# Reordering the 64-key attentions: scores between the two halves of the transposes, keys and queries in a PSUM bank of their own

## The chip, the cores and the metric

One Trainium2 chip, of which the kernel uses one core. The metric is the device time of one execution, in microseconds. The kernel before takes 2080.19 us, the median of 3 runs (2080.02 to 2080.28).

## The reference, cut to what matters

Four layers run over the same 64 batches of 64 tokens of width 128, in float32: a transformer layer with relative positions over 128 keys, a layer with self-attention, cross-attention and feed-forward, a gated fusion with the pooled context, and a layer with self-attention, cross-attention and a mixture of experts. What the change touches are four attentions with 16 heads of 8 channels and 64 keys each:

```
q = heads(q_in, wq, bq)
k = heads(kv_in, wk, bk)
v = heads(kv_in, wv, bv)
scores = jnp.einsum('bhqd,bhkd->bhqk', q, k) / jnp.sqrt(jnp.float32(dh))
attn = jax.nn.softmax(scores, axis=-1)
out = jnp.einsum('bhqk,bhkd->bhqd', attn, v)
```

The first ("msa") and the third ("sa") are self-attentions on the normed tokens; the second ("ca1") and the fourth ("ca") take keys and values from the context. The first and the second have a mask; the third and the fourth have biases on query and key. The output of each is projected and added to the tokens.

## The kernel before, in words

The kernel is one program with phases; each of the five engines has a program of its own, written out by hand, and they meet between phases. Semaphores with counts order the engines within a phase. The four attentions run in two phases of two attentions each (`att_tensor`, `att_vector`, `att_scalar`, `att_pool`, `att_sync`). A tile is two batches of 64 tokens, so 128 partitions; each attention has 32 tiles. `walk_pair` lets both attentions of a phase run on without a break, as a software pipeline: in the step of tile n each engine does, in the order of the code, the `head` work of tile n+2 (norm, transposes, projections), the `front` work of tile n+1 (scores, maximum, shift, exponent), the `back` work of tile n (transposes of the probabilities, product with the values) and the `late` work of tile n-1 (transpose of the context, output projection, addition to X). The steady steps are in a loop of two.

TensorE's order in a step is: the first half of the transposes of tile n's probabilities (`transpose_probs`, line 861, into PSUM bank 4), the second half (bank 5), the mask and scores of n+1 (lines 878 and 883, banks 0 to 3), the transpose of the normed tile n+2 (892) and of its context tile (896 or 899), both into bank 6, the product with the values of n (906, bank 5), the transpose of the context of n-1 (915, bank 6), the products for query, key and values of n+2 (923, 924, 927, all in bank 7), the output projection of n-1 (932, bank 6).

ScalarE copies the two halves of transposed probabilities (1027), the transposed tiles (1039, 1041), computes the first half of the exponents of n+1 (1021), copies the transposed context (1048), the query and the key together (1056 with bias, 1058 without), computes the second half of the exponents, and copies the values (1066).

VectorE norms tile n+2 (962 to 974), finds the maximum (983) and subtracts it (985) in two halves for n+1, takes the reciprocal (990) and multiplies the context (993) of n, adds the projected output to X (999) for n-1 and takes moments (271, 275).

GpSimd makes the mask (830), adds the bias to X (836, 838), and spreads the key over four masked copies (842), which the scores need. SyncE issues the loads of context tiles (805) and masks (809).

## Time and profile before

| what | value |
|---|---|
| median of 3 runs | 2080.19 us |
| the profiled execution | 2078.7 us |
| its span | 2077.1 us |
| busy: TensorE, its weight loads, VectorE, ScalarE, GpSimd | 80%, 62%, 66%, 55%, 46% of the span |
| granted clock of TensorE, mean | 0.905 of full speed |
| line 842 on GpSimd | 128 times, 1048 ns, 299.6 us idle in front of it |
| line 861 on TensorE, transposes | 1024 times, 33.4 us idle in front of them |
| line 983 on VectorE | 256 times, 53.3 us idle in front of it, for the scores |

Busy time leaves out waits and the issuing of DMAs. Idle time is that of the engine just before an instruction, with the engine whose work released it. Times in the rows below are microseconds from the start of the span.

### The profile page before, as it was taken

The numbers are of one execution on the slowest core, as the hardware profiler recorded it, in microseconds if no ns is written. First come the engines' busy times: TensorE is split into PE (matmuls) and PEld (weight loads), VectorE is DVE, ScalarE is ACT, GpSimd is POOL, SyncE is SP. The second block draws the span as 40 slices with busy tenths as digits, with TensorE's granted clock in tenths as the row PEclk, the third lists the DMA queues.
The fourth block names the chain that finished last, engine by engine and source line by source line (L and its number), as shares of the span: only waits on it lengthen the run. The fifth ranks groups of instructions, "written<-read, shape, count | busy, mean of one in ns | idle before, by whom it ended". The sixth has DMA issues, their size and how long they took to land. (4 is left out here: it accounts for less than half of the span.)

```text
span 2077.1 us, 56431 instructions
## 1 busy us (share of the span) xinstructions
PE 1656.3 (80%) x17626; PEld 1290.7 (62%) x17626; DVE 1377.0 (66%) x4296; ACT 1139.2 (55%) x3291; POOL 960.6 (46%) x1443
## 2 busy tenths in 40 slices
PE   5899999999996799998887844599988862219882
PEld 5788888888875666666665721366666651217771
DVE  2677777777775478877776459677777752127783
ACT  1677777777763255566664412377777740007771
POOL 1444444444433344556664424444444434435773
PEclk9999999999998899999998967699999975559996
DMA  6776666666650222210000000000000000016665
GB/s 184 146 161 146 150 145 150 150 152 147 139 127 11 75 88 98 89 52 16 15 15 6 0 1 0 3 0 0 3 11 11 11 5 29 27 51 209 212 221 155
DMA packets 214507, 166.84 MB, mean 80 GB/s; under 512 B 27344, under 2 KB 188496, under 8 KB 214160
## 3 DMA queue, kind: packets, MB, share of 16 engines
q1 hardware_dynamic: 205840, 142.85, 27.5%
q0 software_dynamic: 8576, 22.88, 3.2%
q8 instruction: 45, 0.74, 0.2%
q14 instruction: 46, 0.38, 0.1%
HBM read 91.92 MB, written 73.76 MB: 80 GB/s over the span
## 5 line engine op out<-in xcount | busy, mean ns | idle before, releaser
L842 POOL TENSOR_TENSOR sb_work<-sb_work,sb_cols 128x512 f32<-128x512 f32 x128 | 134.1, 1048 | 299.6 <-ACT sb_work L1056 190.9
L701 ACT ACTIVATE sb_probs<-sb_probs,sb_work 128x128 f32<-128x128 f32 x512 | 198.5, 405 | 112.7 <-DVE sb_work L626 112.7
L983 DVE TENSOR_REDUCE sb_work<-PS 128x8 f32<-128x512 f32 x256 | 175.4, 685 | 53.3 <-PE PS L883 53.3
L280 POOL TENSOR_SCALAR sb_next_var_eps<-sb_next_moments 128x1 f32<-128x1 f32 (+1 forms) x184 | 43.3, 235 | 322.4 <-DVE sb_next_moments L275 322.1
L1021 ACT ACTIVATE sb_work<-sb_work 128x512 f32<-128x512 f32 x256 | 161.2, 630 | 56.2 <-DVE sb_work L985 55.9
L861 PE MATMUL PS<-sb_ident,sb_work 128*128 128x128 f32 x1024 | 165.0, 285 | 33.4 <-ACT sb_work L1021 28.0
L985 DVE TENSOR_TENSOR sb_work<-PS,sb_work 128x512 f32<-128x512 f32 x256 | 177.1, 692 | 8.8
L861 PEld LDWEIGHTS PS<-sb_ident,sb_work 128*128 128x128 f32 x1024 | 114.4, 143 | 68.3 <-ACT sb_work L1021 55.0
L906 PE MATMUL PS<-sb_v_ones,sb_work 128*64 128x18 f32 x4096 | 144.6, 213 | 1.9 <-ACT sb_work L1027 1.8
L906 PEld LDWEIGHTS PS<-sb_v_ones,sb_work 128*64 128x64 f32 x4096 | 132.2, 139 | 19.6 <-issue 7.3
L1027 ACT ACTIVATE sb_work<-PS 128x512 f32<-128x512 f32 x256 | 139.4, 595 | 4.7 <-PE PS L861 1.5
L430 POOL TENSOR_TENSOR sb_work<-sb_rel_bias,sb_work 128x2064 f32<-128x2064 f32 x32 | 134.7, 4211 | 5.2 <-POOL sb_work L428 4.2
L284 POOL TENSOR_TENSOR sb_tile_inv_std<-sb_next_var_eps,sb_half_power 128x1 f32 (+3 forms) x184 | 121.1, 658 | 8.5 <-issue 0.4
L554 PE MATMUL PS<-sb_VO,sb_pkvT 128*128 128x128 f32 x1024 | 119.9, 275 | 0.6 <-ACT sb_pkvT L712 0.6
L554 PEld LDWEIGHTS PS<-sb_VO,sb_pkvT 128*128 128x128 f32 x1024 | 116.9, 192 | 2.7 <-ACT sb_pkvT L712 2.7
L1800 POOL DMA_INDIRECT expert_outs<-sb_work x92 | 94.7, 1029 | 50.4 <-issue 39.7
L535 PE MATMUL PS<-sb_probsT,sb_kv_in 128*128 128x512 f32 x256 | 115.6, 594 | 0.9 <-DVE sb_probsT L648 0.9
L626 DVE CUSTOM_DVE_ANT_0 sb_probs<-PS,sb_work 128x128 f32<-128x128 f32 x512 | 112.4, 285 | 5.6 <-DMA sb_work<-rel_scratch 5.6
L1039 ACT ACTIVATE sb_work<-PS,sb_cols 128x128 f32<-128x128 f32 x128 | 55.1, 455 | 94.0 <-PE PS L899 48.3
L641 DVE TENSOR_TENSOR sb_work<-PS,sb_work 128x512 f32<-128x512 f32 x128 | 82.2, 684 | 34.1 <-PE PS L569 28.9
L701 ACT ACTIVATION_READ_ACCUMULATOR sb_probs<-sb_probs,sb_work 128x1 f32 x512 | 104.1, 203 | 0.0
L734 ACT ACTIVATE sb_work<-PS 128x512 f32<-128x512 f32 x128 | 76.3, 598 | 46.6 <-PE PS L1147 35.8
(274 smaller groups left out, 4477.6 us busy)
## 6 DMA issues: line engine op xcount, KB each, us to landing
rel_scratch<-sb_work SPq DMA_DIRECT2D x64, 516.0 KB, 7.8
sb_work<-rel_scratch SPq DMA_DIRECT2D x64, 512.0 KB, 6.6
expert_rows<-sb_blank SPq DMA_DIRECT2D x36, 520.0 KB, 2.9
sb_w_up<-expert_halves SPq DMA_DIRECT2D x23, 512.0 KB
sb_w_down<-expert_halves SPq DMA_DIRECT2D x23, 512.0 KB
expert_halves<-sb_e_halves POOLq DMA_DIRECT2D x16, 512.0 KB, 5.9
sb_work<-expert_rows SPq DMA_DIRECT2D x23, 260.0 KB
sb_e_raw<-e_W POOLq DMA_DIRECT2D x16, 256.0 KB, 6.7
```

What stands on the lines that cost most here:

```text
L284: e.tensor_tensor(inv_std[:, bass.ds(t0, tiles)], var_eps[:, 0:tiles], half_power[:, 0:tiles], ALU.pow)\
L430: e.tensor_tensor(masked_bias, rel_bias[:, :, :], mask_f.unsqueeze(1).to_broadcast([P, H, KL + 1]), ALU.add)\
L535: e.matmul(PS[:, (j + 1) % 4], kv_in[:, u, b], probsT[:, 8 * G:8 * G + 8, S * b:S * b + S], start=True, stop=True).then_inc(sem("l0_pkv_do ...
L554: ins = e.matmul(PS[:, 3, 0:D], pkvT[:, j], VO[:, j], start=(j == 0), stop=(j == H - 1))
L701: ins = e.activation(probs[:, j], probs[:, j], ACT.Exp, bias=neg_max[:, j:j + 1], scale=-1.0, accum_out=row_sum[:, j:j + 1])
L842: e.tensor_tensor(k_masked[:, u], k_sb[:, u].rearrange("p (b k) -> p b k", b=2).unsqueeze(2) .to_broadcast([P, 2, 4, S]), col("place").uns ...
L861: ins = e.transpose(PS[:, 4 + j, i * P:i * P + P], att_probs[:, u, 8 * j + 2 * i:8 * j + 2 * i + 2], ident[:, :])
L906: ins = e.matmul(values[S * b:S * b + S, 2 * i:2 * i + 2], att_probsT[:, i, S * b:S * b + S], v_ones[:, u, b, 2 * i:2 * i + 2], start=True ...
L983: e.tensor_reduce(top, mine, AX.X, ALU.max).then_inc(sem("att_max_ready"), 1)
L985: e.tensor_tensor(by_group(att_probs[:, v])[:, 2 * j:2 * j + 2], mine, top.unsqueeze(3).to_broadcast([P, 2, 4, S]), ALU.subtract)\
L1021: e.activation(att_probs[:, v, 8 * j:8 * j + 8], att_probs[:, v, 8 * j:8 * j + 8], ACT.Exp, scale=front["scale"]).then_inc(sem("att_exp_do ...
L1027: e.activation(att_probsT[:, 4 * j:4 * j + 4].rearrange("p i q -> p (i q)"), PS[:, 4 + j], ACT.Copy)\
```

## The change

Five edits, of which each moves or splits work and none adds any arithmetic.

1. TensorE: the mask and scores of tile n+1 go between the first and the second half of the transposes of tile n.
2. TensorE: query and key of tile n+2 go into bank 4, the key first, with a count `att_qk_done` of their own behind them; the values stay in bank 7. The bank is shared with the first half of the transposes, so these wait until query and key have been copied.
3. ScalarE copies the key first and the query second when `att_qk_done` says so, each with a count, and waits for the values only before it copies these.
4. GpSimd makes the masked keys after the key's copy; the scores wait for the query's copy as well.
5. TensorE transposes the context of tile n-1 in front of the transposes of tile n+2 and of the product with values; ScalarE copies it in front of the copies of the transposed tiles, and waits until these transposes are done, since they go to the same bank.

```diff
@@ att_pool
-                    e.wait_ge(sem("att_qk_kept"), m + 1)
+                    e.wait_ge(sem("att_qk_kept"), 2 * m + 1)
@@ att_tensor
                 if back:
+                    if front:
+                        e.wait_ge(sem("att_qk_kept"), 2 * n + 4)
                     transpose_probs(n, u, 0)
-                    wait(e, sem("att_ctx_ready"), n)
-                    transpose_probs(n, u, 1)
                 if front:
                     c, m, v = front, n + 1, 1 - u
                     e.wait_ge(sem("att_k_masked"), m + 1)
+                    wait_alone(e, sem("att_qk_kept"), 2 * m + 2)
                     wait(e, sem("att_shifted"), 2 * m)
...
                     ins.then_inc(sem("att_scores_done"), 1)
+                if back:
+                    wait(e, sem("att_ctx_ready"), n)
+                    transpose_probs(n, u, 1)
+                if late:
+                    e.wait_ge(sem("att_ctx_ready"), n)
+                    if head or front:
+                        e.wait_ge(sem("att_T_kept"), n + 2)
+                    wait_alone(e, sem("att_added"), n - 1)
+                    e.transpose(PS[:, 6, 2 * P:3 * P], att_ctx[:, 1 - u], ident[:, :]).then_inc(sem("att_ctxT_done"), 1)
...
-                if late:
-                    e.wait_ge(sem("att_ctx_ready"), n)
-                    if head:
-                        e.wait_ge(sem("att_T_kept"), n + 3)
-                    wait_alone(e, sem("att_added"), n - 1)
-                    e.transpose(PS[:, 6, 2 * P:3 * P], att_ctx[:, 1 - u], ident[:, :]).then_inc(sem("att_ctxT_done"), 1)
                 if head:
...
-                    wait(e, sem("att_qk_kept"), m)
+                    wait(e, sem("att_qk_kept"), 2 * m)
+                    wait(e, sem("att_probsT_kept"), 2 * n + 1 if back else 0)
                     wait(e, sem("att_v_ready"), m)
                     src = yT if cross is None else cT
-                    e.matmul(PS[:, 7, 0:P], wq, yT[:, u], start=True, stop=True)
-                    e.matmul(PS[:, 7, P:2 * P], wk, src[:, u], start=True, stop=True)
+                    e.matmul(PS[:, 4, P:2 * P], wk, src[:, u], start=True, stop=True)
+                    e.matmul(PS[:, 4, 0:P], wq, yT[:, u], start=True, stop=True)\
+                        .then_inc(sem("att_qk_done"), 1)
@@ att_scalar
+                if late:
+                    e.wait_ge(sem("att_ctxT_done"), n)
+                    if head:
+                        e.wait_ge(sem("att_transposed"), n + 3)
+                    wait(e, sem("att_out_done"), n - 2)
+                    e.activation(att_ctxT[:, 1 - u], PS[:, 6, 2 * P:3 * P], ACT.Copy).then_inc(sem("att_ctxT_kept"), 1)
...
-                if late:
-                    e.wait_ge(sem("att_ctxT_done"), n)
-                    wait(e, sem("att_out_done"), n - 2)
-                    e.activation(att_ctxT[:, 1 - u], PS[:, 6, 2 * P:3 * P], ACT.Copy).then_inc(sem("att_ctxT_kept"), 1)
                 if head:
                     c, m = head, n + 2
-                    e.wait_ge(sem("att_projected"), m + 1)
+                    e.wait_ge(sem("att_qk_done"), m + 1)
...
-                    for i, (to, of) in enumerate(((q_sb, PS[:, 7, 0:P]), (k_sb, PS[:, 7, P:2 * P]))):
+                    for i, (to, of) in ((1, (k_sb, PS[:, 4, P:2 * P])), (0, (q_sb, PS[:, 4, 0:P]))):
...
-                    ins.then_inc(sem("att_qk_kept"), 1)
+                        ins.then_inc(sem("att_qk_kept"), 1)
                 if front:
                     exponent(1)
                 if head:
+                    e.wait_ge(sem("att_projected"), m + 1)
```

## Rows read from the trace of the kernel before

**Rows 1.** Timeline, third attention, one step: start, duration, engine, instructions merged
```profile
1434.66 0.69 PE L883 MATMUL PS<-sb_work 32*64 32x256 f32 x16
...
1435.55 1.11 PE L906 MATMUL PS<-sb_v_ones,sb_work 128*64 128x18 f32 x32
...
1436.59 0.33 PE L915 MATMUL PS<-sb_ident,sb_work 128*128 128x128 f32 x1
...
1436.76 0.39 PE L923 MATMUL PS<-sb_work,sb_w_sa 128*128 128x128 f32 x2
...
1436.98 0.39 PE L924 MATMUL PS<-sb_work,sb_w_sa 128*128 128x128 f32 x2
...
1437.30 0.66 PE L927 MATMUL PS<-sb_w_sa,sb_work 128*64 128x128 f32 x8
...
1438.00 0.62 ACT L1056 ACTIVATE sb_work<-PS,sb_cols 128x128 f32<-128x128 f32 x2 [0.30 <-PE PS L927]
...
1438.79 1.05 POOL L842 TENSOR_TENSOR sb_work<-sb_work,sb_cols 128x512 f32<-128x512 f32 x1 [2.82 <-ACT sb_work L1056]
...
1439.20 0.66 PE L861 MATMUL PS<-sb_ident,sb_work 128*128 128x128 f32 x4 [0.39 <-ACT sb_work L1021]
...
1439.63 1.08 ACT L1027 ACTIVATE sb_work<-PS 128x512 f32<-128x512 f32 x2
...
1439.97 0.69 PE L883 MATMUL PS<-sb_work 32*64 32x256 f32 x16
...
1440.59 0.33 PE L892 MATMUL PS<-sb_ident,sb_work 128*128 128x128 f32 x1
```

**Rows 2.** Timeline, first scores of the first attention, TensorE idle until then
```profile
721.13 1.05 POOL L842 TENSOR_TENSOR sb_work<-sb_work,sb_cols 128x512 f32<-128x512 f32 x1
...
722.24 1.04 PE L878 MATMUL PS<-att_mask,sb_ident 128*128 128x256 bf16 x4 [3.86 <-POOL sb_work L842]
```

**Rows 3.** Timeline, first attention, a long step and the ends around it
```profile
759.98 0.69 PE L883 MATMUL PS<-sb_work 32*64 32x256 f32 x16
...
762.13 0.39 PE L923 MATMUL PS<-sb_work,sb_w_msa 128*128 128x128 f32 x2
...
763.90 1.05 POOL L842 TENSOR_TENSOR sb_work<-sb_work,sb_cols 128x512 f32<-128x512 f32 x1 [2.19 <-ACT sb_work L1058]
...
763.99 0.28 DVE L999 TENSOR_TENSOR sb_X<-sb_X,PS 128x128 f32 x1
...
765.18 0.60 PE L878 MATMUL PS<-att_mask,sb_ident 128*128 128x256 bf16 x4
...
765.71 0.69 PE L883 MATMUL PS<-sb_work 32*64 32x256 f32 x16
...
766.88 0.32 PE L892 MATMUL PS<-sb_ident,sb_work 128*128 128x128 f32 x1 [0.49 <-DVE sb_work L974]
...
768.35 0.39 PE L923 MATMUL PS<-sb_work,sb_w_msa 128*128 128x128 f32 x2
...
770.12 0.29 DVE L999 TENSOR_TENSOR sb_X<-sb_X,PS 128x128 f32 x1
```

**Rows 4.** Timeline, second attention, from the projections to the next tile's copies
```profile
1036.20 0.39 PE L923 MATMUL PS<-sb_work,sb_w_ca 128*128 128x128 f32 x2
...
1036.48 0.28 ACT L1048 ACTIVATE sb_work<-PS 128x128 f32<-128x128 f32 x1
...
1039.17 0.33 SPq L805 DMA_DIRECT2D sb_work<-ctx  x1
...
1041.04 0.33 PE L899 MATMUL PS<-sb_ident,sb_work 128*128 128x128 f32 x1 [0.31 <-DMA sb_work<-ctx]
...
1041.56 0.46 ACT L1039 ACTIVATE sb_work<-PS,sb_cols 128x128 f32<-128x128 f32 x1 [1.58 <-PE PS L899]
```

**Rows 5.** Timeline, fourth attention, the copies in front of the projections
```profile
1604.72 0.81 ACT L1039 ACTIVATE sb_work<-PS,sb_cols 128x128 f32<-128x128 f32 x2 [1.00 <-PE PS L896]
...
1605.77 0.45 PE L923 MATMUL PS<-sb_work,sb_w_ca 128*128 128x128 f32 x2
```

## The prediction

> **What bounds the kernel now.** I read the page's shares first: no engine is full over the span, so what counts is the four attentions, 32 tiles each. The rows that group instructions show idle time of TensorE in front of the transposes (line 861), of GpSimd in front of the masked keys (842) and of ScalarE in front of its copies. A sum of idle time says nothing of order, so I went to the timeline of a steady step in each attention. Call P the start of the key and query products (923/924).
>
> In the third attention a step takes 5.31 us, scores to scores [rows 1]. One loop closes on that number: from P 1.20 us until the value products end (1436.76 to 1437.96); 0.04 to the two copies of query and key (1438.00); 1.20 to the second half of the transposes (1439.20), in which ScalarE finishes the pair and computes the second exponent, for which TensorE is idle 0.39; 0.77 to the scores (1439.97), 3.21 so far. Then 0.62 to the next transpose, 0.27 to the product with values (1435.55, 0.89 after the scores at 1434.66), 1.04 to the context transpose, 0.17 to P: 2.10. The sum is 5.31. The reader is to see that the masked keys run beside the second exponent and end at 1439.84, only 0.13 before the scores: the loop has a twin, P to copies to GpSimd to scores, of nearly the same length. VectorE has room here.
>
> The first attention has a short and a long step, 5.73 (scores at 759.98 and 765.71) and 6.22 (P at 762.13 and 768.35). In the long one the transpose of the normed tile (892) waits for VectorE's norm [rows 3]. In the second attention the chain goes through the addition to X, the moments of the context, the load of the next context tile and its transpose (899): P 1036.20, load issued 1039.17, transposed 1041.04 [rows 4]. With 0.26 to the product with values, 1.05 and 0.17 that is 6.32 a step. The fourth alternates too, and its longer step waits for the norm in the same place as the first.
>
> **The change part by part.** Nothing is computed anew; the same instructions change places, three waits are split or added, and no DMA is moved. Each path has to be walked again in the new order: first half of transposes, scores, second half, context transpose, normed tile's transpose, product with values, P, value products, output.
>
> Keys and queries in a bank of their own: ScalarE may copy when line 924's place ends, P+0.61 (1436.98+0.39), not P+1.20; and the key goes first with its own count, so GpSimd starts after one copy, not two. Copies overlap by some 0.10 (0.46 for one of a kind that takes 0.81 for two [rows 4, 5]), so in the pair of 0.62 each lasts 0.36 and holds ScalarE for 0.26; the second costs 0.26. Line 842 moves from P+2.03 to 2.03-0.59-0.26 = P+1.18 and ends at P+2.23 [rows 1]. Before the first scores, when TensorE had nothing else, it started 0.06 after 842 ended [rows 2]. Behind that wait there now stands one more (queries kept) with an instruction of its own, which no row shows. Lower bound 0.06; upper bound 0.28, the 0.11 between transposes and scores (1439.86 to 1439.97) plus the 0.17 that GpSimd took after ScalarE's pair (1438.62 to 1438.79). I take 0.10, since the queries are kept long before, at P+1.27, and only issue remains. Scores start at P+2.33, not P+3.21. Ahead of them on TensorE the first half now waits for the kept queries, about P+1.32; the value products in front of it last until P+1.20 and the output's product comes behind them, so this wait is hidden or nearly so, with nothing to spare: a later copy would delay the first half, and then has some 0.3 of cover until the masked keys come.
>
> Scores between the halves: this takes away the cover that the scores gave to the copy of the second half. From the start of the second half the product with values can't come sooner than 0.66 (transposes) + 0.04 + 0.60 (copy) + 0.05 = 1.35 later; what lies between is the context transpose 0.17 and the normed tile's 0.26, so TensorE stands some 0.2 here [rows 1]. The new loop of the third attention: P+2.33 scores, +0.62 second half, +1.35 product with values, +1.05 P. Together 5.35, against 5.31: the loop is shorter by the exponent and the wait for the value products, and longer by line 842, which ran beside the exponent, and by the copy that has lost its cover. 32 x 0.04 = 1.3 us lost. The exponents are no longer in it: the second is done near P+1.8 and wanted at P+2.95.
>
> In the masked attentions 0.53 us of mask matmuls stand before the scores (765.18 to 765.71), and copies without bias: 842 starts at P+1.77 now (762.13 to 763.90), 0.26 sooner than in the third; since one of the two copies goes, I keep 0.18 of that, an estimate. The loop is 5.35+0.53-0.18 = 5.70; the short step, 5.73 now, therefore stays. The long step goes P, addition +1.77 (768.35 to 770.12), transpose of the normed tile +2.89 (763.99 to 766.88), product with values +0.26, P +1.05: 5.97, against 6.22 [rows 3]. The context transpose has left this path (0.17), and VectorE no longer waits for scores, which come 0.9 sooner. 16 x 0.25 = 4.0 us gained.
>
> Context transposed sooner: it saves 0.17 between the product with values and P, wherever the front of the step sets the pace. But its copy on ScalarE (0.28 at 1036.48, and 0.18 until the next can start, by the 0.10 that copies overlap) now stands in front of the copies of the transposed tiles, and waits until those transposes are done. In the second attention these copies start 0.52 after the last transpose (1041.04 to 1041.56) [rows 4]. The new P is 0.52+0.18+0.36+0.27+0.05 = 1.38 after that transpose; TensorE itself would be ready at 0.26+1.05 = 1.31; now it is 1.48. The gain is 0.10 a step, 32 x 0.10 = 3.2 us. In the fourth attention the two copies scale and add: 0.81 from 1604.72. P = 1604.72+0.18+0.81+0.05 = 1605.76, against 1605.77 [rows 5]: nothing gained, and by the same path nothing in its short step.
>
> A rule of the Trainium skill bears on this (PSUM — Partial Sum Buffer, "PSUM bank collisions raise a hardware error"): two engines may not touch one bank in the same partitions at once, so a copy of the context must not run while TensorE transposes into its bank. That is what the added wait keeps to. Nothing in this trace shows two engines in one bank, so no row bears the rule out or speaks against it. Were the copy free to go ahead, the sum would gain the 2.2 and 4.6 us of rival (b); with the wait it is the one below.
>
> **Sum.** First 4.0, second 3.2, third -1.3, fourth 0: 5.9 us. The profiled execution lasted 2078.7 us with a span of 2077.1; the median is 2080.19, 1.5 above it, and the terms are differences of steps, so I subtract them there: 2074.3. Ends of the attentions give a few tenths at most (the first tile's copies come 0.6 sooner) and are left out.
>
> **The rivals.** (a) *The mask path is longer than I think: slower.* If x is added to the 2.33, the third attention pays 32x, the first's short steps 16x, the fourth's short steps 16 times what exceeds 0.12. The gain is used up at x = 0.12; at the upper bound x = 0.18 it costs 9.6, time 2083.9; a slip of 0.3 would cost 17 and give 2091. For it: both new waits stand directly in this loop, and the queries' wait has no slack. Against it: when TensorE stood idle, it went on within 0.06.
>
> (b) *Larger gain.* ScalarE's copies come through in time: second attention 0.07 x 32 = 2.2, fourth 0.17 x 16 + 0.12 x 16 = 4.6, and with a wait of 0.06 another 1.9. Total 8.7 more, time 2065.6. For it: starts of small copies overlap. Against: the 0.52 seen after the transpose.
>
> (c) *It does nothing that can be measured.* The loads of the second attention and the norm of the first keep their pace: the latter's 4.0 goes, or the second's 3.2, and 2 to 3 us stay: 2077.7. For it: each of the old loops has a twin of nearly equal length. Less than 0.2%, 4.2 us, is about what a measurement can't tell from no change.
>
> (d) *GpSimd holds up VectorE.* Line 842 moves 0.85 sooner, over VectorE's reciprocal, context and addition. In the first attention it ran beside the addition already (763.90 and 763.99) and that took 0.28 as usual [rows 3]; so I give it a twentieth. If it doubled each addition (0.28 more), the norm path would be that much later: some 48 steps, 13 us, time 2088.
>
> **How the numbers follow.** My forecast, 2070 to 2077, has 0.38; (a) 0.20; (b) 0.17; (c) 0.20; (d) 0.05. Faster by over 0.2% (under 2076.0) holds the first and (b), less what of the forecast falls just short: 0.52. Within: (c) and the mild part of (a), 0.27. Slower (over 2084.3): 0.21, the rest of (a), and (d). The forecast's own range is 2070 to 2077. The range goes from (b)'s 2065 to 2086, past the upper bound of (a).
>
> **What would show it.** Right: 842 starts near P+1.0 and P+1.2; scores start 0.1 after it ends; TensorE's idle time in front of the first-half and second-half transposes for ScalarE's exponent is gone, and new idle time stands before the scores (for GpSimd) and before the product with values (for the copies). Steps: first 5.85 on average, second 6.2, third 5.35, fourth 5.78. Wrong: third attention over 5.5 (mask path), or the fourth well under 5.78 (copies), or lines 993 or 999 longer than 0.3.

## The result: slower by 0.85%

The changed kernel takes 2099.26 us (median of 4 runs, 2097.13 to 2101.37), the kernel before 2080.24 beside it; the ratio is 1.0085, with an interval of 1.0066 to 1.0104. The forecast was 2074.3 and the range ended at 2086.0: the sign, the number and the range are all wrong. The profiled execution took 2097.13 us with a span of 2095.5, 18.4 more than before.

From the first scores of each attention to its last (31 steps), from the score rows of both timelines:

| attention | before | after | difference | forecast |
|---|---|---|---|---|
| first | 185.8 us, 5.99 a step | 190.8, 6.15 | +5.0 | -4.0 |
| second | 194.3, 6.27 | 198.1, 6.39 | +3.8 | -3.2 |
| third | 165.6, 5.34 | 175.1, 5.65 | +9.5 | +1.3 |
| fourth | 179.9, 5.80 | 186.3, 6.01 | +6.4 | 0 |

The four sum to +24.7; the stretches before, between and behind them give back 6.3, and 18.4 is left.

Groups of instructions of the kernel after (busy time, mean ns of one, idle time of the engine in front and what ended it):

```profile
L842 POOL TENSOR_TENSOR sb_work<-sb_work,sb_cols 128x512 f32<-128x512 f32 x128 | 134.3, 1049 | 229.9 <-ACT sb_work L1064 154.4
L1033 ACT ACTIVATE sb_work<-PS 128x512 f32<-128x512 f32 x256 | 152.8, 597 | 160.4 <-PE PS L861 156.0
L989 DVE TENSOR_REDUCE sb_work<-PS 128x8 f32<-128x512 f32 x256 | 174.4, 681 | 23.3 <-PE PS L884 23.0
L916 PE MATMUL PS<-sb_v_ones,sb_work 128*64 128x18 f32 x4096 | 142.5, 212 | 33.5 <-ACT sb_work L1033 32.7
L884 PE MATMUL PS<-sb_work 32*64 32x256 f32 x2048 | 91.0, 411 | 16.5 <-POOL sb_work L842 16.5
L879 PE MATMUL PS<-att_mask,sb_ident 128*128 128x256 bf16 x256 | 39.1, 275 | 26.5 <-POOL sb_work L842 26.5
```

By what is idle where, the change did what it says. GpSimd idles 230 us in front of the masked keys, not 299.6; VectorE idles 23 for the scores, not 53.3. TensorE's 33.4 us in front of the transposes have gone (0.8 left), but 33.5 us now stand in front of the product with values (before: 1.9), for ScalarE's copy, and this copy waits 160 us for its transposes (before: 4.7). And a second wait is new: in front of the scores and of the mask's products TensorE idles 16.5 and 26.5 us, all of it for the masked keys; in the kernel before it was 8.2 and 13.0, of which 1.9 and 3.9 for them. The idle time in these four places together went from 56.5 to 77.3 us. Sums of idle time don't show an order, so the step's timeline has to show where the loop went. Third attention of the kernel after:

```profile
1433.02 0.49 PE L928 MATMUL PS<-sb_work,sb_w_sa 128*128 128x128 f32 x2
...
1433.34 0.39 PE L929 MATMUL PS<-sb_work,sb_w_sa 128*128 128x128 f32 x2
...
1433.77 0.62 ACT L1064 ACTIVATE sb_work<-PS,sb_cols 128x128 f32<-128x128 f32 x2 [0.91 <-PE PS L929]
...
1434.21 1.05 POOL L842 TENSOR_TENSOR sb_work<-sb_work,sb_cols 128x512 f32<-128x512 f32 x1 [2.29 <-ACT sb_work L1064]
...
1435.56 0.69 PE L884 MATMUL PS<-sb_work 32*64 32x256 f32 x16 [0.29 <-POOL sb_work L842]
...
1436.18 0.66 PE L861 MATMUL PS<-sb_ident,sb_work 128*128 128x128 f32 x4
...
1436.88 0.60 ACT L1033 ACTIVATE sb_work<-PS 128x512 f32<-128x512 f32 x1 [0.89 <-PE PS L861]
...
1437.62 1.11 PE L916 MATMUL PS<-sb_v_ones,sb_work 128*64 128x18 f32 x32 [0.49 <-ACT sb_work L1033]
...
1438.66 0.49 PE L928 MATMUL PS<-sb_work,sb_w_sa 128*128 128x128 f32 x2
```

Follow P (1433.02) round to the next P (1438.66). 842 starts at P+1.19, where the forecast had 1.18. It ends at 1435.26 and the scores start 0.30 later. Then 0.62 to the second half, 0.70 to its copy, 0.74 to the product with values (0.60 of copy and 0.14 behind it), 1.04 to P. The sum is 5.64, the forecast's was 5.35. This is the forecast's own loop, link by link, with two links that it made too short: 0.10 for the wait behind 842, and 0.05 behind the copy. The wait of 0.30 in this step is a long one. Over 27 steps it is 0.25 on average, and 842 starts at P+1.23 on average; the sum is again 5.64.

First attention, the same loop with the mask's products in it:

```profile
764.89 0.49 PE L928 MATMUL PS<-sb_work,sb_w_msa 128*128 128x128 f32 x2
...
765.99 1.05 POOL L842 TENSOR_TENSOR sb_work<-sb_work,sb_cols 128x512 f32<-128x512 f32 x1 [1.81 <-ACT sb_work L1066]
...
767.44 0.60 PE L879 MATMUL PS<-att_mask,sb_ident 128*128 128x256 bf16 x4 [0.40 <-POOL sb_work L842]
...
767.97 0.69 PE L884 MATMUL PS<-sb_work 32*64 32x256 f32 x16
...
771.07 0.49 PE L928 MATMUL PS<-sb_work,sb_w_msa 128*128 128x128 f32 x2
```

P to P is 6.18 here, forecast 5.70; of the 0.48 the wait has 0.30. Over 27 steps the average is 6.13, which is 0.43 more than forecast: 0.26 in the wait behind 842 (0.36), 0.08 between the start of the second half and the product with values, and 0.10 in front of 842, which starts at P+1.10 where the forecast's sum had 1.00. Every step now runs on this loop, the long ones as the short ones: the 6.22 of [rows 3] came down a little, and the 5.73 went up by 0.4.

In the second attention the early copy of the context works, but not all of its gain arrives:

```profile
1037.79 0.33 PE L909 MATMUL PS<-sb_ident,sb_work 128*128 128x128 f32 x1 [0.37 <-DMA sb_work<-ctx]
...
1038.23 0.28 ACT L1040 ACTIVATE sb_work<-PS 128x128 f32<-128x128 f32 x1 [0.40 <-PE PS L909]
...
1038.77 0.27 ACT L1053 ACTIVATE sb_work<-PS 128x128 f32<-128x128 f32 x1
...
1039.28 0.46 PE L928 MATMUL PS<-sb_work,sb_w_ca 128*128 128x128 f32 x2
```

The context tile is transposed 1.49 before P (forecast 1.38; before, 1.48 in [rows 4]). The last copy ends at 1039.04 and the first product follows 0.24 later, not 0.05. The way from P to the load has grown too: the addition to X starts at P+1.84 (1032.93 to 1034.77), in the kernel before at P+1.77 (1036.20 to 1037.97). The step from P to P is 6.35 here, and the average over the attention 6.39; what lies between these two wasn't followed up.

Last, a thing that the prediction hasn't in any term. Windows of the fourth attention, kernel after (length; busy time and count of TensorE, its weight loads, VectorE, ScalarE and GpSimd; granted clock, where 1.00 is full speed; DMA):

```profile
1618.00:1623.00 5.00, 3.92 (x64) 2.78 (x62) 3.23 (x9) 3.55 (x10) 2.42 (x5) 1.00 0.05 13
1623.00:1627.00 4.00, 4.00 (x34) 2.99 (x34) 1.86 (x7) 2.11 (x7) 1.05 (x1) 0.57 0.00 0
1627.00:1633.00 6.00, 5.50 (x90) 3.82 (x75) 4.53 (x12) 4.66 (x12) 2.58 (x6) 1.00 0.04 11
```

For some 4 us TensorE's granted clock is about half, the lower of its two levels (1.2 GHz and not 2.4); it was idle for 1.1 of the 5.0 us before that. There are four such stretches from 1620 to 1702, and steps in which one begins take 6.7 to 7.3 us. The kernel before has one in its fourth attention, twice as long (at 1533, in a step of 8.12 us). What the four cost is estimated below, from a kernel without them, at 2 to 4 us.

### The profile page after: what moved, and what is told of

Read it like the earlier page. It is cut to its first block and busy times, and to the rows that moved or that the text cites. A ratio compares the mean times of both kernels' runs of the same rounds, so it can differ in the third digit from the quotient of the medians.

```text
span 2095.5 us, 56958 instructions
## 1 busy us (share of the span) xinstructions
PE 1648.3 (79%) x17626; PEld 1293.5 (62%) x17626; DVE 1370.2 (65%) x4296; ACT 1139.1 (54%) x3291; POOL 964.5 (46%) x1443
## 5 line engine op out<-in xcount | busy, mean ns | idle before, releaser
L1033 ACT ACTIVATE sb_work<-PS 128x512 f32<-128x512 f32 x256 | 152.8, 597 | 160.4 <-PE PS L861 156.0
L1027 ACT ACTIVATE sb_work<-sb_work 128x512 f32<-128x512 f32 x256 | 161.7, 632 | 17.0 <-DVE sb_work L991 16.5
L916 PE MATMUL PS<-sb_v_ones,sb_work 128*64 128x18 f32 x4096 | 142.5, 212 | 33.5 <-ACT sb_work L1033 32.7
L884 PE MATMUL PS<-sb_work 32*64 32x256 f32 x2048 | 91.0, 411 | 16.5 <-POOL sb_work L842 16.5
L734 ACT ACTIVATE sb_work<-PS 128x512 f32<-128x512 f32 x128 | 76.2, 598 | 44.7 <-PE PS L1156 34.0
```

The source lines that it names most:

```text
L916: ins = e.matmul(values[S * b:S * b + S, 2 * i:2 * i + 2], att_probsT[:, i, S * b:S * b + S], v_ones[:, u, b, 2 * i:2 * i + 2], start=True ...
L1027: e.activation(att_probs[:, v, 8 * j:8 * j + 8], att_probs[:, v, 8 * j:8 * j + 8], ACT.Exp, scale=front["scale"]).then_inc(sem("att_exp_do ...
L1033: e.activation(att_probsT[:, 4 * j:4 * j + 4].rearrange("p i q -> p (i q)"), PS[:, 4 + j], ACT.Copy)\
```

## Experiments

Each kernel was run beside the kernel before (2080.31, 2078.84 and 2083.53 us in the three sessions), and the ratios are to that. "Half-clock time" below is the time at the lower clock in 735 to 1105 and 1345 to 1675 us of the span. It leaves out one stretch of some 30 us (48 with the scores alone) that every kernel here has just ahead of the third attention (in the kernel before from 1308 to 1339, so outside these windows), and of which a few us fall into the window from 1345 in the slower kernels. Each kernel has one profile, so step lengths and half-clock times are those of one execution.

**The bank alone.** Edits 2 to 4 of the change, with the scores and the context's transpose where the kernel before has them.

```diff
-                    e.matmul(PS[:, 7, 0:P], wq, yT[:, u], start=True, stop=True)
-                    e.matmul(PS[:, 7, P:2 * P], wk, src[:, u], start=True, stop=True)
+                    e.matmul(PS[:, 4, P:2 * P], wk, src[:, u], start=True, stop=True)
+                    e.matmul(PS[:, 4, 0:P], wq, yT[:, u], start=True, stop=True)\
+                        .then_inc(sem("att_qk_done"), 1)
```

> Only keys and queries in their own bank, copied early, key first; both halves of the transposes stay ahead of the scores and the context is transposed where it was. Loop theory (every step is set by one loop of waits, and what the change lost was cover): in the third attention the second exponent now waits only for VectorE's shift, 3.53 us after the scores' start, plus 0.05, 0.63 and 0.05, and the scores follow 0.77 after the second half: a step of 5.03 instead of 5.31, 9 us gained there; 2 us in the first, the second and fourth unchanged: about 2069 us. Rival theory (the bank shared with the first half of the transposes and the added waits are what cost the 18 us): at or above the kernel before, 2080 to 2095 us.

Measured: 2096.76 us, ratio 1.0075 (1.0057 to 1.0094), just above the rival's range. But the loop theory's step came: the third attention is down to 5.10, near the 5.03 expected; yet the whole is slower. The second attention takes 6.80 on average with a median of 6.40. The windows say why:

```profile
735.00:920.00 185.00, 162.59 (x2343) 122.72 (x2342) 144.97 (x363) 113.61 (x308) 93.39 (x185) 0.96 0.23 87
920.00:1105.00 185.00, 160.95 (x2086) 121.06 (x2087) 129.35 (x356) 107.79 (x300) 116.37 (x271) 0.91 0.06 15
1345.00:1510.00 165.00, 148.43 (x2206) 111.40 (x2207) 128.16 (x309) 122.35 (x311) 76.22 (x151) 0.96 0.00 1
1510.00:1675.00 165.00, 145.67 (x2013) 109.68 (x2012) 121.29 (x303) 117.86 (x302) 68.73 (x139) 0.93 0.04 11
```

A clock of 0.91 over 185 us is some 32 us at half speed. The first, second and fourth window hold 70 us in 20 stretches, most of some 4 us. The 0.96 of the third window is something else: it is the end of the long stretch ahead of the third attention, which here runs from 1329 to 1359; the steady steps behind it have the full clock. The kernel before has 1.00, 1.00, 1.00 and 0.98 in these windows. One of the stretches, with the step before it:

```profile
1016.05 0.66 PE L932 MATMUL PS<-sb_w_ca,sb_work 128*64 128x128 f32 x8
...
1018.44 0.69 PE L886 MATMUL PS<-sb_work 32*64 32x256 f32 x16
1020.16 0.32 PE L895 MATMUL PS<-sb_ident,sb_work 128*128 128x128 f32 x1 [1.03 <-DVE sb_work L969]
...
1023.06 1.12 PE L932 MATMUL PS<-sb_w_ca,sb_work 128*64 128x128 f32 x8
...
1026.24 0.69 PE L886 MATMUL PS<-sb_work 32*64 32x256 f32 x16
```

In this step TensorE waits once, for the norm, and its slack is one gap of 1.03 us; in the kernel before the longest gap of a step of this attention is 0.28 in the median and 0.65 at most. Behind it the clock falls, the value products take 1.12 instead of 0.66, and the step is 7.80 long. The gap alone doesn't explain the fall, though: of the ten falls in this attention five come in steps that have two gaps of 0.38 to 0.51 instead, and eight steps with one gap of 0.90 to 1.05 have none.

**The scores alone.** Edit 1 and nothing else.

```diff
                 if back:
                     transpose_probs(n, u, 0)
-                    wait(e, sem("att_ctx_ready"), n)
-                    transpose_probs(n, u, 1)
                 if front:
...
                     ins.then_inc(sem("att_scores_done"), 1)
+                if back:
+                    wait(e, sem("att_ctx_ready"), n)
+                    transpose_probs(n, u, 1)
```

> Only the scores between the two halves of the transposes; keys and queries stay in the values' bank and are copied late. Loop theory: the masked keys end at P+3.08, the scores start 0.3 later, and then 0.62 + 0.70 + 0.74 + 1.04 + 0.17 follow to the next P: 6.65 in the third and fourth attention, 6.97 in the first and second. That is 43 + 28 + 32 + 22 us: about 2205 us. Rival (the mask product is hidden and only the waits' number counts): within 10 us of the kernel before, 2075 to 2090 us.

Measured: 2228.97 us, ratio 1.0707 (1.0681 to 1.0732), 24 above the 2205 expected. The undisturbed steps are 6.85, 6.85, 6.48 and 6.48, somewhat shorter than expected. Third attention:

```profile
1438.23 1.05 POOL L842 TENSOR_TENSOR sb_work<-sb_work,sb_cols 128x512 f32<-128x512 f32 x1 [3.65 <-ACT sb_work L1057]
...
1439.42 0.69 PE L881 MATMUL PS<-sb_work 32*64 32x256 f32 x16 [1.17 <-POOL sb_work L842]
...
1445.89 0.69 PE L881 MATMUL PS<-sb_work 32*64 32x256 f32 x16 [1.16 <-POOL sb_work L842]
```

TensorE stands 1.17 for the masked keys, and steps of 9.2 us at half clock come on top, in the third and fourth attention. So the scores between the halves need the early keys. The wait behind 842 is 0.14 here, and 0.24 in front of the mask's products, with the semaphores of the kernel before.

The second attention of this kernel says something of the clock. TensorE stands 0.82 to 1.01 for the masked keys in every step of the window below, in most of them 1.00:

```profile
980.34 0.60 PE L876 MATMUL PS<-att_mask,sb_ident 128*128 128x256 bf16 x4 [1.00 <-POOL sb_work L842]
```

Its window, with the columns as above:

```profile
920.00:1105.00 185.00, 144.95 (x2096) 106.83 (x2096) 128.33 (x346) 105.21 (x294) 111.39 (x256) 1.00 0.07 20
```

TensorE is idle 40 of these 185 us, the bank alone 24, and yet the clock is 1.00 throughout. Neither a gap of some 1 us in each step nor a smaller share of busy time was enough to bring it down here.

**The context alone.** Edit 5 and nothing else.

```diff
+                if late:
+                    e.wait_ge(sem("att_ctx_ready"), n)
+                    if head or front:
+                        e.wait_ge(sem("att_T_kept"), n + 2)
+                    wait_alone(e, sem("att_added"), n - 1)
+                    e.transpose(PS[:, 6, 2 * P:3 * P], att_ctx[:, 1 - u], ident[:, :]).then_inc(sem("att_ctxT_done"), 1)
                 if head:
```

> Only the context transposed and copied sooner. Loop theory: the context transpose in front of P hid 0.10 of the loading of the first weights, so moving it takes 0.07 and not 0.17 out of the path from the product with values to P, while it adds its 0.17 ahead of the normed tile's transpose where the scores set the pace: third attention 5.41 (+3 us), the others within 1 us each: about 2083 us. Rival (the copy of the context in front of the copies of the transposed tiles is what costs most): the second and fourth attention slower by 0.1 to 0.2 a step, 2088 us or more.

Measured: 2074.15 us, ratio 0.9969 (0.9957 to 0.998): faster by 0.31%, where 2083 was expected. Steps 5.92, 6.20, 5.37 and 5.78 on average. The second attention's 6.20 is the forecast's 6.2, the first's long step came from 6.22 to 6.11, and the other two are what they were. No half-clock time. Here P follows the last copy of the transposed tiles after 0.05 us wherever TensorE waits for it, the forecast's figure; this kernel doesn't have the wait that edit 2 adds in that place.

**The masked keys' wait put last.** The whole change, with the order of the waits in front of the scores turned round.

```diff
-                    e.wait_ge(sem("att_k_masked"), m + 1)
-                    wait_alone(e, sem("att_qk_kept"), 2 * m + 2)
+                    e.wait_ge(sem("att_qk_kept"), 2 * m + 2)
                     wait(e, sem("att_shifted"), 2 * m)
                     if c["mask"]:
                         e.wait_ge(sem("att_mask_ready"), m + (c["mi"] - c["i"]) * NT + 1)
+                    wait_alone(e, sem("att_k_masked"), m + 1)
```

> The whole change, but TensorE waits for the kept queries, the shift and the mask first and for the masked keys last, in an instruction of its own, so that nothing stands behind the wait that ends last. Theory (the 0.30 to 0.35 between the end of line 842 and the scores is the issuing of the waits behind it): that gap falls to 0.15 or less, steps of the third attention from 5.64 to 5.45 or so, 16 to 20 us less in all attentions bound by it with the second less: 2086 to 2092 us. Rival (the gap is the way of GpSimd's signal to TensorE): gap and time unchanged, 2097 to 2100 us.

Measured: 2096.89 us, ratio 1.008 (1.0061 to 1.0099). Expected were 2086 to 2092, so the time missed. From the end of 842 to TensorE's next product, medians of the third and of the first attention: 0.14 and 0.24 in the kernel before, 0.24 and 0.36 in the whole change. Here it takes two values in turn, step by step: 0.14 and 0.25 in the third, 0.10 and 0.25 in the first. A step of the short kind:

```profile
1440.04 1.05 POOL L842 TENSOR_TENSOR sb_work<-sb_work,sb_cols 128x512 f32<-128x512 f32 x1 [2.34 <-ACT sb_work L1065]
...
1441.23 0.69 PE L885 MATMUL PS<-sb_work 32*64 32x256 f32 x16
```

So in every second step the order of the waits is worth 0.10 us in the third attention and 0.26 in the first, and in the others nothing in the third and 0.10 in the first; why every second step keeps 0.25 is open. On average the wait went from 0.25 to 0.20 and from 0.36 to 0.17. The third attention's steps followed, 5.65 to 5.61, and the first's only in part, 6.15 to 6.03, since in the steps with the short wait the product with values waits longer (0.28 behind the copy, not 0.14). The time fell by 2 us, within the intervals. The order of the waits is a part of the loss, and a small one.

**The bank alone, with unread work in the gap.** As the first experiment, and four transposes of the identity behind the scores in the first, second and fourth attention, into a place of bank 7 that nobody reads then. They change no result.

```diff
+                    if head and back and c["i"] != 2:
+                        e.wait_ge(sem("att_v_ready"), m + 1)
+                        for i in range(4):
+                            e.transpose(PS[:, 7, 0:P], ident[:, :], ident[:, :])
```

> The bank-only kernel with four transposes of the identity, that nobody reads, on TensorE behind the scores in the first, second and fourth attention, written to the free quarter of bank 7. Work is added, none taken away. Clock theory (in the bank-only kernel all of TensorE's slack of a step stands in one gap of 1.03 us in front of the normed tile's transpose, and behind such a gap the granted clock falls to the lower level for some 4 us; 23 such stretches are what made it slower): with about 0.5 us of the gap filled the stretches are gone, and what is left are the steps, 5.94, 6.37, 5.07 and 5.85: about 2076 us, 20 us less than without the added work. Rival (the shared bank and the waits cost the time, and the clock only follows): no fewer stretches, and the time rises by the added work where it stands in the loop, 2097 to 2110 us.

Measured: 2074.11 us, ratio 0.9969 (0.9957 to 0.9981): 22.6 us less than without, by adding work, and near the 2076 expected. The windows that answer to those above:

```profile
735.00:920.00 185.00, 177.45 (x2523) 133.61 (x2522) 149.86 (x373) 115.87 (x315) 96.05 (x191) 1.00 0.24 87
920.00:1105.00 185.00, 172.90 (x2315) 129.03 (x2313) 135.00 (x375) 112.53 (x316) 123.07 (x289) 0.99 0.06 16
1345.00:1510.00 165.00, 152.94 (x2357) 116.61 (x2357) 136.23 (x328) 128.34 (x327) 78.67 (x160) 1.00 0.01 2
```

The medians of the steps are those of the kernel without these transposes within 0.1 us (6.38 and 6.40 in the second attention, 4.94 in both in the third); what has gone are the slow steps. Two stretches of half clock are left, 7 us in all, where there were 20. The third window, whose own attention got no such transposes, rose from 0.96 as well only because this kernel is ahead by then: its long stretch runs from 1309 to 1340 and ends before the window.

**Bank and context, scores not moved**, and **the same with the four transposes**. Edits 2 to 5 without edit 1.

> The change without its reordering of the scores: own bank and early copies, context transposed sooner, both halves of the transposes ahead of the scores. Loop theory, by the sum of the two parts measured alone (16.5 slower and 6.2 faster): 2090 us, with a step of 5.1 in the third attention and stretches at the lower clock as in the bank-only kernel, fewer if the context transpose, now inside the gap, splits it. If the reordering of the scores is what costs most of the change's 18 us beside the clock, this kernel beats the whole change; if not, it stands at 2097 or above.

Measured: 2084.73 us, ratio 1.0024 (1.0013 to 1.0034); steps 5.91, 6.72, 5.02, 6.04 and 62 us at half clock. The whole change differs from this kernel in edit 1 alone and takes 14.5 us more.

> The kernel of own bank and context sooner, with the same four unread transposes behind the scores. Clock theory: no stretches at the lower clock in the attentions except at their ends, steps of 5.9, 6.25, 5.1 and 5.8: about 2070 us, the fastest of all. Rival (the clock falls whatever the gaps): 2085 us or more.

Measured: 2067.58 us, ratio 0.9937 (0.9923 to 0.9951); steps 5.85, 6.45, 5.02, 5.83 and 7 us at half clock. Faster by 0.63% than the kernel before, and by 1.5% than the kernel after.

**The whole change with unread work.** Three such transposes behind the early transpose of the context, where it waits for ScalarE's copy.

```diff
+                    if head and back:
+                        e.wait_ge(sem("att_v_ready"), n + 2)
+                        for i in range(3):
+                            e.transpose(PS[:, 7, 0:P], ident[:, :], ident[:, :])
```

> The whole change with three unread transposes of the identity behind the context transpose, where TensorE waits for the norm or for the copy of the second half. Clock theory: the four stretches of some 4 us at the lower clock in the fourth attention go, which is about 4 us, and the steps stay, since the added 0.35 us lies beside waits of 0.5 to 0.6: 2094 to 2097 us. Rival (the change's loss is mostly the clock): 2080 to 2085 us.

Measured: 2094.82 us, ratio 1.0069 (1.0055 to 1.0083), as expected; no half-clock time, steps 6.14, 6.37, 5.65, 5.94. Mostly the fourth attention moved (from 6.01, 2.3 us over its 31 steps). The medians differ by 4.4 us, and the intervals overlap. So the clock holds at most some 4 us of the whole change's loss, and the other 15 are in its steps.

**Half the masked keys**, in the whole change and in the kernel before. Line 842 makes the masked keys of a tile's first batch only, and the scores of both batches are computed from them; the second batch's own keys are left out.

```diff
-                    e.tensor_tensor(k_masked[:, u], k_sb[:, u].rearrange("p (b k) -> p b k", b=2).unsqueeze(2)
-                                    .to_broadcast([P, 2, 4, S]),
-                                    col("place").unsqueeze(1).unsqueeze(3).to_broadcast([P, 2, 4, S]), ALU.mult)\
+                    e.tensor_tensor(k_masked[:, u, 0], k_sb[:, u, 0:S].unsqueeze(1).to_broadcast([P, 4, S]),
+                                    col("place").unsqueeze(2).to_broadcast([P, 4, S]), ALU.mult)\
...
-                            ins = e.matmul(scores[S * b:S * b + S, g], q_sb[r, v, S * b:S * b + S], k_masked[r, v, b],
+                            ins = e.matmul(scores[S * b:S * b + S, g], q_sb[r, v, S * b:S * b + S], k_masked[r, v, 0],
```

> The whole change, with line 842 making the four masked keys of a tile's first batch only (256 elements in each partition in place of 512, so some 0.5 us shorter); the scores of both batches use them, so the scores of the second batch are computed from the first batch's keys. Loop theory: in the whole change the step is one loop, products, copy of the key, masked keys, scores, second half, copy, product with values. Then cutting 0.5 us out of line 842 shortens the third attention's step from 5.64 until the next limit, 4.9 to 5.15, the first's short step from 6.13 to about 5.7, the second's hardly (6.3), the fourth's to about 5.8: in all some 25 us, time 2072 to 2080. Rival (the splits and added waits cost their own time, whatever the masked keys take): steps within 0.1 us of the whole change's, time 2092 to 2100.

Measured: 2093.12 us, ratio 1.0044 (1.0029 to 1.0058). Third attention:

```profile
1434.70 0.69 PE L883 MATMUL PS<-sb_work 32*64 32x256 f32 x16
...
1437.80 0.49 PE L927 MATMUL PS<-sb_work,sb_w_sa 128*128 128x128 f32 x2
...
1438.99 0.62 POOL L842 TENSOR_TENSOR sb_work<-sb_work,sb_cols 128x256 f32<-128x256 f32 x1 [1.90 <-ACT sb_work L1063]
...
1439.40 0.65 PE L860 MATMUL PS<-sb_ident,sb_work 128*128 128x128 f32 x4
...
1439.98 0.69 PE L883 MATMUL PS<-sb_work 32*64 32x256 f32 x16
```

842 lasts 0.43 less and the step is 5.28, 0.36 less than 5.64; the rival, that the added waits themselves cost the time, wanted no change. The next limit comes sooner than expected: the masked keys end at 1439.61, but TensorE issues the first half of the transposes at P+1.60 and needs 0.58 for it, so the scores can't start before P+2.18. The first attention's steps went from 6.15 to 5.86. The time, though, missed its 2072 to 2080 by far, because there are now some 27 us at half clock in the second attention (6.65 on average, median 6.31) and 31 in the fourth, up to 1700; the third has none. That was not foreseen in the expectation, in spite of the first experiment.

> The same cut of line 842 in the kernel before, nothing else changed. Loop theory: there the masked keys run beside the second exponent, which ends its own path to the scores at nearly the same time, so the cut gives next to nothing: third attention 5.25 to 5.35 a step (now 5.31), time 2077 to 2081. If line 842 was the limit in the kernel before as well, the third attention would come down to 5.1 or less and the time to 2070 or less.

Measured: 2077.27 us, ratio 0.9974 (0.9954 to 0.9994). Third attention:

```profile
1435.37 0.62 POOL L842 TENSOR_TENSOR sb_work<-sb_work,sb_cols 128x256 f32<-128x256 f32 x1 [2.86 <-ACT sb_work L1055]
...
1436.37 0.69 PE L882 MATMUL PS<-sb_work 32*64 32x256 f32 x16
...
1441.68 0.69 PE L882 MATMUL PS<-sb_work 32*64 32x256 f32 x16
```

5.31 as before, with the masked keys ready 0.38 ahead of the scores. The same cut that takes 0.36 off a step of the changed kernel takes nothing off this one: in the kernel before 842 lay beside the exponent, and the change put it on the only path. The first and the fourth attention gained 1.6 and 3.3 us; the fourth's may be the clock, since the one long step of the kernel before (8.12 us, at half clock) is missing here.

**A mix.** Context sooner in all four attentions; own bank, key first and early copies only in the first and third; scores not moved. Then the same with the four unread transposes in the first attention.

```diff
+                    early = head["i"] in (0, 2)
...
+                    if early:
+                        e.matmul(PS[:, 4, P:2 * P], wk, src[:, u], start=True, stop=True)
+                        ins = e.matmul(PS[:, 4, 0:P], wq, yT[:, u], start=True, stop=True)
+                    else:
+                        e.matmul(PS[:, 7, 0:P], wq, yT[:, u], start=True, stop=True)
+                        ins = e.matmul(PS[:, 7, P:2 * P], wk, src[:, u], start=True, stop=True)
```

> Own bank, early copies and key first only in the first and third attentions; context transposed sooner in all four; scores where the kernel before has them. The aim is the short third attention (about 5.0 a step) without the lower clock that the own bank brought in the second. Steps 5.9, 6.2, 5.0, 5.8: 2062 to 2070, some half-clock stretches possible in the first attention. If the clock falls in the first as it did in the second with the bank in all, 2070 to 2078.

Measured: 2072.72 us, ratio 0.9945 (0.9925 to 0.9965); steps 5.90, 6.35, 5.02, 5.95; some 10 us at half clock. A gain, 3 us short of the first expected range, since the second attention didn't keep the 6.20 it has with the context alone (it goes 6.54 and 6.25 in turn) and the fourth takes 5.95, not 5.8. The instructions of the second are the same; what differs are the counts it waits on and how it follows on the first. This stays open.

> The kernel of the run before with four more transposes behind the scores in the first attention, into a bank place that nobody reads; they go where TensorE waits anyway. Clock theory: any half-clock stretches of the first attention go, its steps 5.85, time 2060 to 2066. If there were none to begin with: the same time within 2 us or up to 2 us more.

Measured: 2069.89 us, ratio 0.9928 (0.9904 to 0.9953); no half-clock time up to 1675, the first attention at 5.84 as expected, the time 4 us above the expected 2060 to 2066. The interval overlaps those of the mix without unread work and of bank, context and unread transposes (0.9923 to 0.9951): these three are the best versions, 0.55 to 0.7% faster than the kernel before, and nothing here tells them apart.

## Why the prediction was wrong

**Right: where each loop goes.** The loop of the third attention is the predicted one link by link, P, key's copy, masked keys, scores, second half, its copy, product with values, P; 842 starts at P+1.19 against 1.18 (1.23 on average). Halving 842 in both kernels showed it to be on the path that sets the step after the change, and covered before it. Also right is the idle time that was to vanish and to appear. Of two errors in the 1.18, one made good the other: the key and query products take 0.32 and 0.39, not 0.22 and 0.39, since the context's transpose no longer stands in front of them (in the kernel with the context alone they start 0.32 apart too), and what follows was 0.09 shorter.

**Wrong: "I take 0.10, since the queries are kept long before, at P+1.27, and only issue remains."** Measured 0.30 in the step shown, 0.24 and 0.36 as medians of the third and first attention. The upper bound was 0.28. The 0.10 leant on [rows 2], TensorE idle for 3.86 us, and passed over [rows 3], in which the mask's products start at 765.18 and 842 ends at 764.95: 0.23, from a steady step, in a row that was quoted. That row alone doesn't prove the price, since TensorE's transposes ran until 765.05; the scores alone, where TensorE stood idle for 1.00 before it, show the same 0.24. So 0.14 and 0.24 is what the kernel before pays in steady steps, and the added wait brings 0.10 and 0.12 more. The queries are indeed kept long before; the wait on them costs all the same, because it stands behind the one that comes last: with that one put last the time falls to 0.14 and 0.10 in every second step. In the third attention's step shown this is 0.20 of the 0.29 by which the loop was mis-sized, and 0.15 on average.

**Wrong: 0.05 behind a copy that TensorE waits for.** The second half's copy cost 0.66+0.04+0.60+0.05 in the forecast. The product with values starts 0.14 after its end (the median of 30 steps), and 1.44 after the second half; that is another 0.09. No row of the prediction shows the 0.05 for this place. Behind the copy of the transposed tile, where a wait has been added too, it is 0.24 (0.05 in the kernel with the context alone, which doesn't have that wait), and takes the forecast's 0.10 a step from the second attention. In the kernel with the context alone 0.07 of them came.

Put in the forecast's own sums, rival (a)'s x, which is what the loop takes more than forecast, is 0.29 in the third (31 x 0.29 = 9.0, with the 1.3 foreseen 10.3; measured 9.5). In the first it is 0.43 on average, since the estimate "I keep 0.18 of that" was 0.10 too much as well; it lifts the mask's loop to 6.13, above the 5.97 of the norm's, so that the gain of 4.0 became a loss of 5.0. This is rival (a), at 0.20 and 2083.9 to 2091: the rival was right and its price too low, because the wait behind 842 was bounded at 0.28, the one behind the copy had no bounds at all, and (a) left the second attention out, which turned from a gain of 3.2 into a loss of 3.8. The loops of the second and the fourth attention (+6.4) weren't taken apart link by link.

**Missing: TensorE's clock.** No term and no rival had it; the table ahead of the prediction shows 0.905, but nearly all of that lies outside the attentions, where the kernel before has 1.00, 1.00, 1.00 and 0.98. In the whole change it is a small matter, at most 4 us. In the parts it decides the sign: the bank alone goes from 2074.11 to 2096.76 and bank with context from 2067.58 to 2084.73 where the unread transposes are taken out. With such transposes in both, edit 1 costs 2094.82 - 2067.58 = 27 us on top of the others; without them in either, 14.5.

**The other rivals.** (b) and (c) didn't come: in the kernel with the context alone, where the mask's path is as before, the second attention gained 2.0 of its 3.2, the first 2.2 of 4.0. (d) is refuted: the multiplication of the context (999) and the addition (1005) still take at most 0.293 and 0.289.

What the whole change got wrong as an idea follows. Edit 5 alone is a gain of 0.31%. Edits 2 to 5 together are a gain of 0.63% with unread work on TensorE, and a loss of 0.24% without. Edit 1 on top costs 14.5 to 27 us: it puts the masked keys with both hand-overs on the only path, and takes from the second copy the scores that covered it. The forecast weighed all five together against the kernel before, and didn't ask what the step would be without edit 1: the same walk along [rows 1], with edits 2 to 4 only, would have priced the short third attention that the bank alone showed (5.10).

The Trainium skill (Perfetto Trace Analysis, "Per-engine timelines") says that the way of a semaphore update to the other engines comes after the reported end of an instruction and is not in the profile. The trace agrees in so far as no product here followed the copy or the masked keys that it waited for sooner than 0.05 us after their end.

## What to carry to other kernels

Price every hand-over (from the end of one engine's instruction to the start of the one that waited for it on another engine) by the gap seen in steady steps in the same place of the code with the same waits, not by one seen elsewhere: between ScalarE's copies and TensorE alone it was 0.05, 0.14 or 0.24 us here. Try writing last the wait that comes last. When an edit consists of parts, forecast each subset: here one part of five cost 14.5 to 27 us, whatever the other four did. And when TensorE's waits move, look at the granted clock of each stretch: half-clock stretches cost more here than the waits that were taken out, and unread work in TensorE's gaps won that back.

## What the runs showed of the hardware

TensorE's clock fell to half in steady loops in which TensorE was never idle for more than 1.5 us at a time. With the bank alone the granted clock was 0.91 in the second attention, in the kernel before 1.00. What brings it down isn't shown. One gap of 1.03 us stands before some of the falls, two gaps of 0.38 to 0.51 before others, and 0.54 with 0.29 before the four in the whole change. With the scores alone a gap of 0.82 to 1.01 us in every step of the second attention brought none. The share of busy time doesn't tell them apart either: TensorE was busy 161.0 of 185 us with the bank alone (its slow stretches among them), 164.9 in the kernel before, 161.3 in the whole change and 145.0 with the scores alone, and the clock of the last three was 1.00 there. That TensorE's idle time has a part in it is what the unread transposes bear out: with them 20 stretches became two, and the time fell. The Trainium skill (TensorE: Matmul & The Clock Gate, Part 1) says that a monitor of TensorE's activity sets the clock to full or half, and the stretches agree with two levels (1.00, or about 0.5 inside a stretch).

Adding four transposes a step that nobody reads made two kernels faster by 22.6 and 17.2 us. In the whole change three of them gave 4.4, near the width of its interval.

The order of waits on one engine, all but one of them long fulfilled, changed the time from a GpSimd instruction's end to TensorE's start: from 0.36 to 0.10 us in every second step of the first attention, and to 0.25 in the others.
